# Transposes of a quartet's first-layer values as one DMA, and the second product one tile behind the first

## The reference, cut to what matters

```python
def simple_rms_norm(x):
    return x / jnp.maximum(jnp.linalg.norm(x, axis=-1, keepdims=True), 1e-12) * jnp.sqrt(d)

def activation_quant(x):
    scale = 127.0 / jnp.clip(jnp.max(jnp.abs(x), axis=-1, keepdims=True), EPS)
    return jnp.clip(jnp.round(x * scale), -128, 127) / scale

def bitlinear158(x, w):        # w: rounded to -1, 0, 1 times one scale
    return jnp.einsum('bsi,oi->bso', activation_quant(simple_rms_norm(x)), weight_quant(w))

h = gelu(bitlinear158(layernorm(x), w1))      # 512 -> 2048
h = gelu(h)
x = x + tanh(g_ffn[0]) * bitlinear158(h, w2)  # 2048 -> 512
```

## Time and profile before

| | |
|---|---|
| median of 3 runs | 1078.73 us (1076.58 to 1078.87) |
| the profiled execution | 1076.09 us |
| its span, first to last instruction | 1074.2 us |
| TensorE busy | 937.0 us (87%) |
| VectorE busy | 713.6 us (66%) |
| ScalarE busy | 558.8 us (52%) |
| GpSimd busy | 502.2 us (47%) |
| granted TensorE clock, mean | 0.957 of full speed |
| ternary loop, first product to last add | 156.86 to 297.55 us |

### The profile page before, as it was taken

The page is one execution under the profiler, slowest core; times in us unless marked ns, Lnnn a source line. Parts: engine busy times, 40 slices in busy tenths (PEclk is TensorE's granted clock), DMA queues, the critical chain, the costliest instruction groups (busy, mean ns, idle before and its releaser), DMA issues. The chain is left out here.

```text
span 1074.2 us, 17065 instructions
## 1 busy us (share of the span) xinstructions
PE 937.0 (87%) x5251; PEld 420.9 (39%) x5252; DVE 713.6 (66%) x1403; ACT 558.8 (52%) x849; POOL 502.2 (47%) x538
## 2 busy tenths in 40 slices
PE   0467679899788989999999898899999999999995
PEld 0333334344332322333333223344445555556542
DVE  6988987789768776777776765777353344333347
ACT  5897989778427767767666672534131111111120
POOL 1100335564323577566566661104716887870065
PEclk9988889899888999999999999889999999999997
DMA  8422892446633533331311232996643889956588
GB/s 326 143 79 78 259 248 42 89 92 107 126 99 85 133 90 101 96 85 53 98 64 47 76 62 89 210 340 222 235 153 89 216 201 215 224 133 155 139 315 291
DMA packets 238591, 158.49 MB, mean 148 GB/s; under 512 B 176772, under 2 KB 205444, under 8 KB 238008
## 3 DMA queue, kind: packets, MB, share of 16 engines
q1 hardware_dynamic: 229576, 128.57, 45.1%
q0 software_dynamic: 8080, 27.60, 7.9%
q10 hardware_dynamic: 864, 1.44, 0.4%
HBM read 73.03 MB, written 44.02 MB: 109 GB/s over the span
## 5 line engine op out<-in xcount | busy, mean ns | idle before, releaser
L1836 DVE CUSTOM_DVE_ANT_0 ajunk<-p_row,mask_row 128x512 bf16<-128x512 f32 x256 | 166.1, 685 | 69.6 <-PE p_row L1660 61.9
L1571 ACT ACTIVATE prob<-p_pair,mask_col,any_key 128x512 f32<-128x512 f32 x168 | 121.8, 774 | 65.0 <-PE p_pair L1715 64.6
L1660 PE MATMUL p_row<-ks,early_place 99*128 99x512 f16 x256 | 100.9, 398 | 13.5 <-DVE top L1836 12.7
L1715 PE MATMUL p_pair<-early_place,ks 101*128 101x512 f16 x256 | 98.1, 388 | 6.0 <-ACT prob L1571 4.8
L3018 DVE SCALAR_TENSOR_TENSOR shid<-p_pair,ssilu 128x352 f32<-128x352 f32 x36 | 18.9, 524 | 93.8 <-PE p_pair L2923 93.8
L1571 ACT ACTIVATE early_place<-p_pair,mask_col,any_key 128x512 f32<-128x512 f32 x88 | 64.1, 774 | 31.2 <-PE p_pair L1715 30.8
L2938 PE MATMUL s_down<-mw,shT 128*128 (+5 forms) x396 | 75.8, 379 | 0.5 <-DMA shT<-shidr 0.5
L593 PE MATMUL po<-w2T,ctxT 128*128 128x512 f16 x256 | 61.4, 397 | 15.3 <-DMA ctxT<-w 15.3
L2852 ACT ACTIVATE ssilu<-s_gate 128x352 f32<-128x352 f32 x36 | 16.7, 463 | 108.6 <-PE s_gate L2923 108.6
L2923 PE MATMUL s_gate<-mw,spare 128*128 (+1 forms) x504 | 66.6, 313 | 1.3 <-DMA spare<-x_slots 1.2
L2923 PE MATMUL p_pair<-mw,spare 128*128 (+1 forms) x504 | 66.4, 312 | 0.0
(11 more groups left out here) (451 smaller groups left out, 2199.6 us busy)
## 6 DMA issues: line engine op xcount, KB each, us to landing
x_slots<-nought SPq DMA_DIRECT2D x6, 1536.0 KB, 14.3
y_slots<-spare SPq DMA_DIRECT2D x36, 256.0 KB, 2.3
early_place<-in_ctx SPq DMA_DIRECT2D x8, 1024.0 KB, 5.7
early_place<-halves_d SPq DMA_DIRECT2D x45, 128.0 KB, 2.4
halves_d<-halves SPq DMA_DIRECT2D x18, 256.0 KB, 2.0
x<-in_x SPq DMA_DIRECT2D x4, 1024.0 KB, 7.4
w<-in_L_ffn_w SPq DMA_DIRECT2D x1, 4096.0 KB, 17.9
w<-in_L_ffn_w SPq DMA_DIRECT2D x4, 1024.0 KB, 4.9
```

The lines of the kernel that those rows point to most:

```text
L1571: nc.scalar.activation(prob_of(KB * blk + k, pr)[:, c, :], p_col[c][:], ACT.Exp, bias=mask_col[:, b, k:k + 1], scale=any_key[:, b:b + 1]). ...
L1660: nc.tensor.matmul(p_row[n % 2][:], qs[0:ROWS_R, j, g, t * P:(t + 1) * P], ks[b % 2][0:ROWS_R, g, :], start=True, stop=True).then_inc(t_ro ...
L1715: nc.tensor.matmul(p_col[c][:], ks[b % 2][0:ROWS_C, g, k * P:(k + 1) * P], qs[0:ROWS_C, j, g, :], start=True, stop=True).then_inc(t_col, 1)
L1836: nc.vector.tensor_tensor_reduce(junk[:, n % 2, :], p_row[n % 2][:], mask_row[:, blk // HPG, :], 1.0, -3e38, ALU.add, ALU.max, top[blk % 2 ...
```

## The change

`turn_in` takes a group, not a tile, and issues one DMA transpose for it: 128x512 for tile 0, 128x1536 for tiles 1 to 3, 128x2048 for a quartet. For that the values of a quartet lie in one piece: they are written into the second half of the other buffer, and transposed into the first half of their own. VectorE gets waits that keep the two apart (`normalise`, and `quantise` of tile 0). The first two transposes are issued ahead of `load_last`, the wait for the clearing of x_slots moves to the end of SP's program, and so do the four transposes of x. The second product runs one tile behind the first, and VectorE's adds with it.

```diff
-    q1, q1T = ([t.rearrange("p t (h c) -> p t h c", h=2)[:, :, :, n * P:(n + 1) * P].bitcast(F16) for t in (y[0][:], y[1])] for n in range(2))
+    q1, q1T = ([t.rearrange("p t d -> p (t d)")[:, n * QUARTET * D // 2:(n + 1) * QUARTET * D // 2].bitcast(F16) for t in places]
+               for n, places in ((1, (y[1], y[0][:])), (0, (y[0][:], y[1]))))
...
-            sp.wait_ge(s_quant, 2 * B - 1)
-            early.load_last(sp)
-            sp.wait_ge(b_clear, 16 * 6)
-
-            def turn_in(t):
-
-                sp.wait_ge(b_q1, t + 1)
-                need(sp, b_turn1[t % QUARTET], 32 * (t // QUARTET))
-                g, i = t // QUARTET % 2, t % QUARTET
-                for n in range(2):
-                    sp.dma_start_transpose(q1T[g][:, i, n, :].rearrange("p (k n) -> p k n", n=P), q1[g][:, i, n, :]).then_inc(b_turn1[i], 16)
+
+            def turn_in(g):
+
+                a, b = GROUPS_OF[g]
+                sp.wait_ge(b_q1, b)
+                sp.dma_start_transpose(columns_of(a, b - a), values_of(a, b - a)).then_inc(b_turn1[g], 16)
...
-            for t in range(*GROUPS_OF[0]):
-                turn_in(t)
-            for t in range(*GROUPS_OF[1]):
-                turn_in(t)
+            turn_in(0)
+            turn_in(1)
+            sp.wait_ge(s_quant, 2 * B - 1)
+            early.load_last(sp)
             for t in range(NT + 1):
                 if t >= 1:
                     turn_hidden(t - 1)
                 if AHEAD.get(t, (None,))[0] == 3:
-                    for i in range(*GROUPS_OF[AHEAD[t][1]]):
-                        turn_in(i)
+                    turn_in(AHEAD[t][1])
...
-                if t == NT - 2:
-                    sp.wait_ge(b_xrows, 2)
-                    for i in range(TPB):
-                        early.turn(sp, early.xT, keep, i, early.t_xt)
+            sp.wait_ge(b_xrows, 2)
+            for t in range(TPB):
+                early.turn(sp, early.xT, keep, t, early.t_xt)
+            sp.wait_ge(b_clear, 16 * 6)
...
-                if t == 2:
+                if t == 1:
                     pe.wait_ge(s_added, RESIDUALS)
-                if t >= 2:
-                    product_hidden(t - 2)
-            for t in range(NT - 2, NT):
-                product_hidden(t)
+                if t >= 1:
+                    product_hidden(t - 1)
+            product_hidden(NT - 1)
...
+                for n in ((), (), (0, 1), (2,), (3,))[g]:
+                    dve.wait_ge(b_turn1[n], 16)
...
+                if g == 0:
+                    dve.wait_ge(s_prod, TPB * (B - 1))
                 dve.wait_ge(b_k1, g + 1)
...
-                if t >= 3:
-                    add(t - 3)
+                if t >= 2:
+                    add(t - 2)
```

More of the change, by code:

```diff
@@ L227, in stage_cross_ternary @@
         sem("b_" + n) for n in ("gelu1", "gelu2", "hsq", "hmax", "k2", "a2", "q2", "prod2", "added", "gate"))
-    b_turn1, b_turn2 = ([sem(f"b_turn{m}_{n}") for n in range(count)] for m, count in ((1, QUARTET), (2, 2)))
+    b_turn1, b_turn2 = ([sem(f"b_turn{m}_{n}") for n in range(count)] for m, count in ((1, len(GROUPS_OF)), (2, 2)))
     b_xv, b_xr, b_ctxrows, b_xrows = (sem("b_" + n) for n in ("xv", "xr", "ctxrows", "xrows"))
@@ L234, in stage_cross_ternary, with columns_of, values_of @@
     AHEAD = {(a - 6 + n): (n, g) for g, (a, b) in enumerate(GROUPS_OF) if g > 1 for n in range(4)}
-    def columns_of(t):
-        return [q1T[t // QUARTET % 2][:, t % QUARTET, k // 2, k % 2 * P:(k % 2 + 1) * P] for k in range(KB)]
+    def columns_of(t, n=1):
+        return q1T[t // QUARTET % 2][:, t % QUARTET * D:(t % QUARTET + n) * D].rearrange("p (k n) -> p k n", n=P)
+    def values_of(t, n=1):
+        return q1[t // QUARTET % 2][:, t % QUARTET * D:(t % QUARTET + n) * D]
     with nc.Block() as block:
@@ L580, in product_in @@
                 if n == 0:
-                    pe.wait_ge(b_turn1[t % QUARTET], 32 * (t // QUARTET + 1))
+                    pe.wait_ge(b_turn1[group_of(t)], 16)
                 need(pe, b_gelu1, 2 * (t - 1) + n + 1)
@@ L584, in product_in @@
                     for k in range(KB):
-                        mm = nc.tensor.matmul(ph[n][:, c:c + D], columns_of(t)[k], w1T[:, k, n * HALF + c:n * HALF + c + D],
+                        mm = nc.tensor.matmul(ph[n][:, c:c + D], columns_of(t)[:, k, :], w1T[:, k, n * HALF + c:n * HALF + c + D],
                                               start=(k == 0), stop=(k == KB - 1))
@@ L780, in quantise @@
                 a, b = GROUPS_OF[g]
+                if g == 0:
+                    dve.wait_ge(s_prod, TPB * (B - 1))
                 dve.wait_ge(b_k1, g + 1)
                 for t in range(a, b):
-                    nc.vector.tensor_scalar(q1[t // QUARTET % 2][:, t % QUARTET], y_of(t).rearrange("p (h c) -> p h c", h=2), k1[:, t:t + 1], TINY, ALU.mult, ALU.mult).then_inc(b_q1, 1)
+                    nc.vector.tensor_scalar(values_of(t), y_of(t), k1[:, t:t + 1], TINY, ALU.mult, ALU.mult).then_inc(b_q1, 1)
             PIECES = (statistics, normalise, largest, quantise)
@@ L955, in _ @@
             quantise_hidden(NT - 1)
-            add(NT - 3)
+            add(NT - 2)
             kv_low()
-            add(NT - 2)
             add(NT - 1)
```

## The result

| | before | changed |
|---|---|---|
| median | 1078.87 us (5 runs, 1076.58 to 1081.39) | 1085.12 us (5 runs, 1082.90 to 1086.72) |
| ratio | | 1.006, 95% interval 1.0037 to 1.0083 |
| profiled execution, its span | 1076.09, 1074.2 us | 1085.12, 1082.5 us |
| first product of the loop starts | 156.86 | 158.84 |
| first product of tile 15 starts | 271.43 | 281.09 |

The account below looks back on a forecast made before the run. Bound: TensorE waiting for transposed hidden values behind eight narrow transposes on SP's queue. Tile 15's first product at 271.43 - 0.6 - 11.4 + 3.45 + 13.4, plus 22.5 and 1.0 for the clock: +2.3 us, 1081.0 us, range 1071 to 1089.

Parts of the forecast that it names:

- One transpose for a quartet: SP's queue: one wide transpose issues in 1.45 us, lands in 4.5; TensorE's three long waits and a slow group go, -11.4 us.
- the sign: What would show the forecast on SP's queue: single wide transposes of under 2 us; 5 us or more would refute it.
- the walk: The loop carried through with measured durations, each engine in its own order, giving TensorE's waits ahead of tiles 0 to 12.
- The start: Loop start on TensorE: first two transposes issued ahead of the weight loads save between 0 and 0.8 us, taken as -0.6.
- One more second product ahead of tile 15: TensorE: with the second product one tile behind, one more stands ahead of tile 15's first product, +3.45 us.
- new waits of 13.4: TensorE, second products of tiles 0 to 12: hidden values ready at a + 17.8 against a slot of a + 17.3, +13.4 us.
- the slow group: TensorE behind tile 12's 4.0 us wait: clock may be lost, costing 1.9 us; half counted, 1.0 us.
- The end: From tile 15's first product to the last add: 22.5 us against 26.1, nothing given to moving the x transposes.
- A: Rival: data in time, only 3.5 of 13.4 us of waits remain; 1070 us, shown by ctxT waits under 8 us; chance 0.22.
- B: Rival: hand-over from transpose issue to TensorE's start takes 4.4 us, not 4.8; 2.1 us off, 1078.9 us; chance 0.11.
- C: Rival: on TensorE each of eight waits over 0.5 us is followed by a slow group of 1.9; 1096 us; chance 0.07.
- D: Rival: wide transpose paid by width, 10.8 us of SP issue ahead of tiles 1, 5, 9; 1108 us; chance 0.05.

Follow-up runs that it names:

- the repeat: The changed kernel and the kernel before, both run again unaltered: ratios to before 1.0022 and 1.0008, loops 145.6 and 141.5 us.
- the lag of two: Changed kernel with its second product two tiles behind the first again: ratio to before 0.9878, loop 134.1 us; run again 0.9886, 132.2 us.

## Why the prediction was right, and where its size was off

**What bounds the kernel: right.** TensorE waited for transposed hidden values behind eight narrow transposes. With them gone and the lag kept, no second product up to tile 6 waited and the loop fell by 6.6 and 8.5 us.

**One transpose for a quartet, -11.4 us: right**, though its price was not. The issue took 2.55 to 3.03 us for 128x2048 in the first profile, not the 1.45 taken nor the under 2 us of the sign; my step was that width costs next to nothing from 256 to 1024, and it did not go on to 2048 there. Width alone does not set it either: the 128x512 one of tile 0 took 2.89 us. Landing of all five is 4.4 us at the median, and of the three wide ones 4.3 to 4.8, as the 4.5 said:

```profile
L273 SPq DMA_TRANSPOSE keep<-xT x3: 1421/2553/2892, 145.0 to 211.4; - x3
L273 SPq DMA_TRANSPOSE xT<-keep x2: 2610/2821/3032, 179.9 to 242.6; - x2
...
DMA to landing us min/median/max: 3.7/4.4/7.6
```

The dearer issue shows in waits of 1.0, 1.4 and 1.6 us ahead of tiles 1, 5 and 9, where the walk had 0.1, 0.5 and 0.5; the tiles behind then wait less (tile 6 under 0.2, where 1.4 was forecast). SP had less than the 1.9 us free that I said: tile 5's transposes were issued 0.9 us late.

**The start, -0.6 us: right in kind.** The first product starts 0.06 us behind VectorE's last copy (158.10 + 0.68), not 0.8 as in the earlier trace rows. The copy itself came 2.7 us later, since the clock was lower between 76 and 88 us.

**One more second product ahead of tile 15, +3.45, and new waits of 13.4.** The waits that the profile names up to tile 12 sum to 12.6 us. Tile 15's first product came 122.25 us after the first of all, 7.7 more than before (114.57), and 7.7 = -11.4 + 3.45 + 12.6 + 1.7 + 1.4, where 1.7 is the slow group and 1.4 is what is left. The starts of the groups place it: a group behind a named wait starts some 0.16 us later than the wait alone makes it, ten times against three before, and tiles 4 and 6 start 0.1 and 0.2 us late without a named wait. The walk had 13.4 against these 14.0. Tile by tile it was further off (1.8, 1.4 and 1.8 us ahead of tiles 2, 6 and 10, where the profile has 0.4, 0.2 and 0.4, and less than measured ahead of 1, 5, 9 and 11), so that the sum came out to 0.6 us is in part luck. The cause that it named is there: quantising began 12.5 us behind the tile's own first product for tile 8, but 13.3 and 14.7 for tiles 6 and 7 (206.68 to 219.95, 213.68 to 228.38), beside which the pieces of the next quartet stand. Its terms as listed add to 13.5. **The slow group** behind tile 12's wait was counted at half, 1.0; it came, with 1.7, and 2.8 when the kernel ran again (6.41 us for 16 matmuls). **The end, 22.5 us:** 22.7 in both profiles, but not with nothing given to the transposes of x: ahead of tile 14 they made it 24.2.

So by its own steps, from the first product to the last add, the sum was +2.8 and the runs show +4.3: 0.6 from the waits, 0.7 from the clock, 0.2 from the end. The two profiled spans lie 8.3 us apart, and the other 4.0 are none of the steps: 2.0 us ahead of the loop and 2.0 behind the barrier, which the repeat did not show. The medians lie 6.3 us apart in the first comparison and 2.4 (by the ratio) in the repeat; that the one forecast, 2.3, is so near to the second is luck as well, since the loop itself took 4.2 or more in both. The mechanism and its place held; the loop's loss was about half again as large as forecast. The term that was most too small is the slow group: 1.0 us counted, 1.7 and 2.8 measured, behind waits of 3.33 and 3.97.

**The rivals.** A (data in time) fell: 12.6 us of waits, not under 8. B (a shorter hand-over) held in part and did not decide: from the issue to TensorE's start took 4.5, 4.6 and 4.7 us for tiles 1, 5 and 9, where the walk had 4.8 and B 4.4, the hidden transposes landed in 3.3 us as before, and the waits were no fewer. C (the clock goes with every wait) fell: groups behind waits up to 1.6 us took 3.6 us. D (paid by width) fell as a rival: 1.9 to 3.0 us over the two profiles and not 10.8. Two of its figures were off: at half the price its own sum is three times 5.4 less 1.9, 10.5 us and not 13; and C counted eight waits over 0.5 us where the walk has seven, 13 us and not 15.

## What to carry to other kernels

Slack that seems unused in a steady stretch can be what hides work done once in four tiles; before a product is moved one tile nearer to its input, lay the whole chain from one to the other in microseconds against the slot, with the extra pieces of each engine in it. Here 17.8 us stood against 17.3, and the pieces for the next quartet made each miss larger. Of two edits made together, run each alone: one was worth 7 to 9 us and the other took 11 to 13. A lag of one tile less puts one more product ahead of the last tile and takes one from behind it: against before the way to tile 15 got 3.45 us longer by it, the end 3.4 us shorter. And compare the length of the stage that was changed, not only the whole: one pair of spans lay 8.3 us apart where the loops lay 4.3 apart.

## What the runs showed of the hardware that was not expected

A DMA transpose of 128x1024 holds SP's queue about 1.3 us, hardly more than one of 128x256, and one of 128x1536 took 1.42. One of 128x2048 took between 1.8 and 3.3 us in the nine profiles that had it; the first of the stretch was near 3.0 in six of them and the last at 1.8 to 2.0 in eight. The 128x512 one of tile 0, the first behind the clearing of x_slots, took 2.4 to 5.3 us in the ten profiles that had it, as much as a wide one or more. I have no cause for either.

Ahead of the second products, TensorE's clock stayed at 2.4 GHz through waits of up to 2.8 us; at longer ones it was not settled by the wait's length alone: waits of 3.20 and 3.67 us left the group behind them at full speed (3.61 us), in the lag of two and its repeat, and others of 3.24, 3.27, 3.33 and 4.19 did not (1.3 to 2.8 us more). At the start of the loop, where TensorE had last done short transposes, the first product ran wholly or mostly at the lower clock in all 13 profiles, behind waits of 2.7 to 3.8 us: 3.2 to 3.6 us, where the same group takes 1.9 later on.

And the same f32 group took 3.6 to 6.3 us in profiles whose code is identical up to it, the loop's start lay anywhere within 3.6 us, and the loop's own length moved by over 1 us with the clock of its first two product groups.
